# Attention on one core: probability sums moved behind the next group's value products, through a score-row bank and two sum buffers

## The reference

```python
x = x + xattn(layernorm(x), ctx, ctx)     # q (16,112,1024), k and v (16,375,256)
#   scores = q k^T / sqrt(32);  probs = softmax(scores);  out = (probs v) Wo
x = x + ffn(layernorm(x))                 # (silu(x w1^T) * (x w3^T)) w2^T
```

## Time and profile before

| | us |
|---|---|
| median of three executions (lowest, highest) | 2510.83 (2504.62, 2513.42) |
| span of the profiled execution, first to last instruction | 2511.5 |
| PE busy in that span | 2424.5 (97%) |
| DVE busy | 1727.6 (69%) |
| ACT busy | 979.1 (39%) |
| POOL busy | 576.1 (23%) |

### The profile page before, as it was taken

The page is one execution under the profiler, slowest core; times in us unless marked ns, Lnnn a source line. Parts: engine busy times, 40 slices in busy tenths (PEclk is TensorE's granted clock), DMA queues, the critical chain, the costliest instruction groups (busy, mean ns, idle before and its releaser), DMA issues.

```text
span 2511.5 us, 35414 instructions
## 1 busy us (share of the span) xinstructions
PE 2424.5 (97%) x12682; PEld 2069.3 (82%) x12682; DVE 1727.6 (69%) x2639; ACT 979.1 (39%) x1673; POOL 576.1 (23%) x305
## 2 busy tenths in 40 slices
PE   7998999999999699799999999999999989999999
PEld 7997878878876388699999988998899978888887
DVE  6425777777776446788888889898889874445442
ACT  3212445444454422444444445344443342323221
POOL 1000354454454400011111111332333320000000
PEclk9998999999998799899999999999999999999999
DMA  7534555455545345465655554666676687565652
GB/s 225 174 96 135 146 135 146 131 142 143 133 113 130 86 155 168 126 203 168 186 170 168 165 151 148 181 180 183 194 211 182 172 284 228 170 186 151 186 163 84
DMA packets 369146, 408.04 MB, mean 162 GB/s; under 512 B 125824, under 2 KB 324096, under 8 KB 359152
## 3 DMA queue, kind: packets, MB, share of 16 engines
q1 hardware_dynamic: 369008, 406.22, 56.7%
HBM read 252.99 MB, written 152.70 MB: 162 GB/s over the span
## 4 chain that ended last, share of the span: by engine, by line
PE 44%; DVE 9%; issue 3%; DMA 2%; ACT 0%; DVEq 0%; ACTq 0%
PE bank L84 15%; PE bank L85 15%; PE bank L86 15%; DVE g_WL L90 2%; DMA stash<-weight_scratch 2%; DVE g_su L1731 1%; DVE stash L1736 1%; DVE g_XL L90 1%; DVE stash L1228 1%; DVE stash L1226 1%; DVE xT L1723 1%; DVE stash L1225 1%; DVE stash L1249 0%; ACT g_XH L1659 0%; ACT g_WH L1198 0%
## 5 line engine op out<-in xcount | busy, mean ns | idle before, releaser
L84 PE MATMUL bank<-g_XH,g_WH 128*128 128x448 f32 (+1 forms) x2254 | 847.1, 376 | 30.2 <-DVE g_XL L90 15.9
L86 PE MATMUL bank<-g_XH,g_WL 128*128 128x448 f32 (+1 forms) x2254 | 845.0, 375 | 0.0
L85 PE MATMUL bank<-g_XL,g_WH 128*128 128x448 f32 (+1 forms) x2254 | 844.9, 375 | 0.0
L84 PEld LDWEIGHTS bank<-g_XH,g_WH 128*128 128x128 f32 x2254 | 424.5, 188 | 93.7 <-DVE g_WL L90 18.1
L86 PEld LDWEIGHTS bank<-g_XH,g_WL 128*128 128x128 f32 x2254 | 424.6, 188 | 55.3
L85 PEld LDWEIGHTS bank<-g_XL,g_WH 128*128 128x128 f32 x2254 | 424.7, 188 | 54.3
L90 DVE TENSOR_TENSOR g_WL<-stash,g_WH 128x512 fp32r<-128x512 f32 (+1 forms) x417 | 349.3, 841 | 75.8 <-ACT g_WH L1198 47.1
L1198 ACT ACTIVATE g_WH<-stash 128x512 fp32r<-128x512 f32 x392 | 241.7, 628 | 398.9 <-PE bank L86 245.1
L696 DVE TENSOR_REDUCE a_nm<-bank 112x1 f32<-112x375 f32 x512 | 264.9, 531 | 117.1 <-PE bank L831 113.8
L800 ACT ACTIVATE a_pr<-bank 125x448 f32<-125x448 f32 x384 | 204.0, 545 | 204.4 <-PE bank L907 150.8
L649 POOL TENSOR_TENSOR a_prsum<-a_pr 125x1792 f32<-125x1792 f32 x32 | 129.3, 4042 | 363.0 <-ACT a_pr L800 363.0
(11 more groups left out here) (132 smaller groups left out, 3617.8 us busy)
## 6 DMA issues: line engine op xcount, KB each, us to landing
stash<-in_L_ffn_w SPq DMA_DIRECT2D x168, 256.0 KB, 5.2
weight_scratch<-stash SPq DMA_DIRECT2D x28, 1024.0 KB, 7.6
stash<-weight_scratch SPq DMA_DIRECT2D x28, 1024.0 KB, 5.4
h_scratch<-g_Sh SPq DMA_DIRECT2D x112, 224.0 KB, 2.8
down_scratch<-xT SPq DMA_DIRECT2D x98, 256.0 KB, 3.0
stash<-in_ctx SPq DMA_DIRECT2D x48, 500.0 KB
stash<-h_scratch SPq DMA_DIRECT2D x25, 896.0 KB, 6.4
a_qst<-q_scratch SPq DMA_DIRECT2D x96, 224.0 KB, 4.7
```

The lines of the kernel that those rows point to most:

```text
L84: pe.matmul(acc, lh, rh, start=first, stop=False, skip_group_check=onto)
L85: pe.matmul(acc, lh, rl, start=False, stop=False, skip_group_check=onto)
L86: return pe.matmul(acc, ll, rh, start=False, stop=last, skip_group_check=onto)
```

## The change

- The sums of group 1 of the batch before are made in step 19, straight behind the value products of group 0; the sums of group 0 in step 31, straight behind those of group 1. On POOL's side `prsum` becomes two buffers, one per group, the second in a free part of `stash`.
- The sums go to `bank[1]`, one of the two score banks. Heads from 21 on swap banks, so that head 20 and head 31 sit in bank 0 when the sums are made. Heads 0 and 21 now wait for the head just before them, and heads 1 and 22 for `copy_sums`.
- ACT: `copy_sums` of group 0 goes to step 0 of the next turn, ahead of `copy_out` of group 1; that of group 1 to step 20, ahead of exponential 14 and `copy_out` of group 0.
- DVE inverts group 0's sums in steps 5, 8, 11, 14 of the next turn, group 1's in steps 22, 23, 25, 27.
- POOL scales group 0 of the batch before between the two adds of group 0, and group 1 behind them.
- SP: the store of group 0 goes behind the six loads of group 0's stacks (and so behind the `Wo` loads in turn 14), the store of group 1 behind the six loads of group 1's. The first load of the next stage waits for all sums, since its target overlaps the second `prsum`.

```diff
-                o_bank = l_bank = bank[6]
+                o_bank, l_bank = bank[6], bank[1]
-                SUMS = {2: (1, 1), 22: (0, 0)}
-                INV = {25: (0, 0), 27: (0, 1), 28: (0, 2), 31: (0, 3),
-                       5: (1, 0), 8: (1, 1), 11: (1, 2), 14: (1, 3)}
+                SUMS = {19: (1, 1), 31: (0, 0)}
+                HEAD_AFTER_SUMS = HEADS[19][-1] + 1
+                INV = {5: (0, 0), 8: (0, 1), 11: (0, 2), 14: (0, 3),
+                       22: (1, 0), 23: (1, 1), 25: (1, 2), 27: (1, 3)}
+                def head_bank(h):
+                    return s_bank[(h + (h >= HEAD_AFTER_SUMS)) % 2]
...
-                            if attn and not (isinstance(b, int) and b == 0):
-                                store(b - 1, 0)
                             if not isinstance(b, int) or -2 <= b < B - 4:
...
                                 load_stacks(i, par, b, 0)
                             if attn and not (isinstance(b, int) and b == 0):
-                                store(b - 1, 1)
+                                store(b - 1, 0)
                             if proj:
                                 load_stacks(i, par, b, 1)
+                            if attn and not (isinstance(b, int) and b == 0):
+                                store(b - 1, 1)
...
                         sp.wait_ge(pv_done, NC * NG * (B - 1))
+                        sp.wait_ge(sums_done, NG * B)
                         load_tile(sp, 0)
...
                                 add(b, 0, 0)
-                                if not (isinstance(b, int) and b == 0):
+                                if later:
+                                    scale(b - 1, 0)
+                                add(b, 0, 1)
+                                if later:
                                     scale(b - 1, 1)
-                                add(b, 0, 1)
                                 add(b, 1, 0)
                                 add(b, 1, 1)
-                                scale(b, 0)
...
-                                if attn and s == 1 and not (isinstance(b, int) and b == 0):
+                                if attn and s == 0 and not (isinstance(b, int) and b == 0):
+                                    copy_sums(b - 1, 0)
                                     copy_out(b - 1, 1)
-                                if attn and s - 1 in SUMS:
-                                    g, back = SUMS[s - 1]
-                                    if not (isinstance(b, int) and b < back):
-                                        copy_sums(b - back, g)
+                                if attn and s == 20 and not (isinstance(b, int) and b == 0):
+                                    copy_sums(b - 1, 1)
...
-                            pe.wait_ge(o_copied, NG * b + g + 1)
...
-                                                 prsum[:, r, :], start=True, stop=True)
+                                                 prsum[g][0:CK, r, :], start=True, stop=True)
...
-                                    wait(pe, max_done, NH * sb_ + h - 1)
+                                    wait(pe, max_done, NH * sb_ + h - (h not in (0, HEAD_AFTER_SUMS)))
+                                    if attn and h == 1:
+                                        wait(pe, l_copied, NG * b - 1)
+                                    if attn and h == HEAD_AFTER_SUMS + 1:
+                                        wait(pe, l_copied, NG * b)
...
                                     g = PV[s]
-                                    wait(pe, l_copied, NG * b + g)
+                                    wait(pe, o_copied, NG * b + g)
...
+                                    sg, back = SUMS[s]
+                                    if not (isinstance(b, int) and b < back):
+                                        if score:
+                                            pe.wait_ge(max_done, NH * sb_ + (20 if sg else NH - 1))
+                                        else:
+                                            pe.wait_ge(max_done, NH * (b + 1))
+                                        sums(b - back, sg)
```

More of the change, by code:

```diff
@@ L450, in attention @@
                 v = stash[0:CK, 8:10, 0:NC * KV].rearrange("p s (c n) -> p s c n", c=NC)
-                pr, prsum = sb("pr", [P, R, NC, J * SQ]), sb("prsum", [CK, R, J * SQ])
+                pr = sb("pr", [P, R, NC, J * SQ])
+                prsum = (sb("prsum", [CK, R, J * SQ]),
+                         stash[0:CK, 10:12, :].rearrange("p a n -> p (a n)")[:, 0:R * J * SQ]
+                         .rearrange("p (r n) -> p r n", r=R))
                 o, l = sb("o", [P, NG, J * SQ]), sb("l", [P, NG, J * SQ])
@@ L641, in add @@
                             n = NG * b + g
+                            acc = prsum[g][0:CK, :, :]
                             pool.wait_ge(exp_done, R * (NC * n + 2 + last))
@@ L644, in add @@
                                 pool.wait_ge(two_added, n + 1)
-                                pool.tensor_tensor(prsum[:], prsum[:], pr[0:CK, :, 2, :], ALU.add
+                                pool.tensor_tensor(acc, acc, pr[0:CK, :, 2, :], ALU.add
                                                    ).then_inc(all_added, 1)
                             else:
-                                wait(pool, sums_done, n)
-                                pool.tensor_tensor(prsum[:], pr[0:CK, :, 0, :], pr[0:CK, :, 1, :],
+                                wait(pool, sums_done, n - 1)
+                                if isinstance(b, int) and b == 0 and g == 1:
+                                    pool.wait_ge(w_lo, KT)
+                                pool.tensor_tensor(acc, pr[0:CK, :, 0, :], pr[0:CK, :, 1, :],
                                                    ALU.add).then_inc(two_added, 1)
@@ L661, in body @@
                             if attn:
+                                later = not (isinstance(b, int) and b == 0)
                                 add(b, 0, 0)
-                                if not (isinstance(b, int) and b == 0):
+                                if later:
+                                    scale(b - 1, 0)
+                                add(b, 0, 1)
+                                if later:
                                     scale(b - 1, 1)
-                                add(b, 0, 1)
                                 add(b, 1, 0)
                                 add(b, 1, 1)
-                                scale(b, 0)
                         each(pool, body)
+                        scale(B - 1, 0)
                         scale(B - 1, 1)
@@ L729, in body @@
                                                           ).then_inc(v_moved, 1)
[L730 to L735, removed]
+                                if attn and s in INV and not (isinstance(b, int) and b == 0):
+                                    invert(b - 1, *INV[s])
                         each(dve, body)
-                        for j in range(J):
-                            invert(B - 1, 1, j)
+                        for g in range(NG):
+                            for j in range(J):
+                                invert(B - 1, g, j)
                     @block.scalar
@@ L805, in _ @@
                         each(act, body)
+                        copy_sums(B - 1, 0)
                         copy_out(B - 1, 1)
@@ L910, in body @@
                                               ).then_inc(st_done, 1)
-                                if attn and s in SUMS:
-                                    g, back = SUMS[s]
-                                    if not (isinstance(b, int) and b < back):
-                                        sums(b - back, g)
                                 if attn and s in PV:
                                     g = PV[s]
-                                    wait(pe, l_copied, NG * b + g)
+                                    wait(pe, o_copied, NG * b + g)
                                     pe.wait_ge(v_moved, b + 1)
```

7 lines of the change are left out of this document (5 added, 2 removed).

## The result

The changed kernel takes **2588.32 us** (median of four runs, 2586.47 to 2593.84); the kernel before took 2510.97 us in four runs (2504.62 to 2513.42). The ratio is **1.0325, 95% interval 1.0307 to 1.0343**: slower by 77 us, 9 us less than forecast, inside the range. The profiled execution spans 2592.1 us, 80.6 more than before. The sum came out, but its terms did not: stall 1 was put too high and the clock far too low, and these errors cancelled in part.

A forecast was written before the change was run, and what follows sets the result against it. PE alone was taken to set the pace in attention's full turns. Terms 0 + 50 + 17 + 10 + 9 = 86 us, on the profiled 2511.5 us and less 0.7 for the median, gave 2597 us, range 2565 to 2640.

The forecast's parts named there:

- stall 1: Step 20, turns 1 to 12: group 0's `copy_out` waits for the late store, delaying head 26 by 4.2 us; 50 us.
- the clock: Turns 1 to 12: PE's idling brings half-clock stretches costing 1.7 us each; half of twelve, 10 us, bounds 0 and 40.
- stall 2: Step 0, turns 2 to 12: group 1's `copy_out` waits for its store, delaying head 6 by 1.5 us; 17 us.
- What the sums cost: Sums on PE, two per turn: 2.1 us falls to 1.64 behind the value products, gaining 0.46 us a turn.
- Heads 1 and 22: Heads waiting for `copy_sums`: head 1 loses 0.5 us, head 22 nothing, cancelling the sums' gain; 0 us a turn.
- POOL, DVE and the second buffer: Group 1's adds some 4 us later, covered by more than 5 us; attention's last load costs 0 to 1 us.
- the chain: Turn 8: store landing, `copy_out`, context copy, low part, maxima and inversion lead to head 26, 11.7 us behind the products' start.
- issued at 586.23: Turn 8: group 0's moved store, behind six loads, issues at 586.23 and lands 5.6 us later, at 591.8.
- The last turns: Turn 14: group 0's store behind the 32 `Wo` loads makes `copy_out` 9.3 us later; +9 us, bounds 0 and 12.
- only part of the halt reaches PE: Rival: PE feels ACT's halt through exponentials alone, 2 us in twelve turns, no clock loss; 2545 us, chance 0.22.
- Faster: Rival: group 0's store lands 2.4 us after issue, in time for step 20's `copy_out`; 2502 us, chance 0.07.
- No difference: Rival: PE slack absorbs the late copies, or waits removed at the end pay for half the stalls; 2511, chance 0.05.

The follow-up runs named there:

- x1: The changed kernel with group 0's store right behind the context load and POOL's scale of group 0 ahead of group 0's adds; 2542.8 us, ratio 1.0143.
- x3: The changed kernel with the edits of x1 and x2 together, so both stores early; 2524.67 us, ratio 1.0071.
- x5: The changed kernel with a second output buffer for group 0, by the batch's parity, all queue places kept; 2545.65 us, ratio 1.0154.
- x12: The changed kernel with x1's early store, a second output buffer for group 1, and group 1's inversions in steps 24, 25, 27, 28; 2502.71 us, ratio 0.9994.
- x13: x12 with head 1 of the next item moved behind step 1's projections; 2502.06 us, ratio 0.9982.
- x6: The kernel before with the context load issued ahead of group 0's store; 2503.05 us, ratio 0.9999.
- x2: The changed kernel with group 1's store ahead of the six loads of group 1's stacks; 2589.9 us, ratio 1.0331.
- x8: x3 with group 1's inversions in steps 24, 25, 27, 28 instead of 22, 23, 25, 27; 2532.8 us, ratio 1.0100.
- x10: x8 with both stores issued by POOL right behind its scaling; 2541.6 us, ratio 1.0139.

## Why the prediction was right, and where its terms were not

The total and its cause were right: 2597 forecast, 2588.32 measured, and experiments x1, x3, x5 and x12 show that the moved stores and what follows from them make nearly the whole loss, the rest being the inversions in steps 22 and 23. That the number came so close is in part luck: stall 1 was 17 us too high, the clock 22 us too low, stall 2 7 us too low. Against x12, which has the sums in the same place without the store waits and with the inversions spread, the twelve turns of the changed kernel split into idle time, 56.4 - 4.0 = 52.4 us, and the clock, 483.97 - 452.32 = 31.7 us. By the steps:

- **What the sums cost.** Forecast gain 0.46 us a turn, measured 5.1 / 12 = 0.42. Right. From the sums' start to the next head's they take 637.21 - 636.34 = 0.87 us.
- **Heads 1 and 22.** Forecast: head 1 loses 0.5 us and cancels that gain. Measured 3.2 / 12 = 0.27 in x12, and x13, which covers it, is 0.26 us a turn shorter. A wait on the weight load of up to 0.6 lies mostly beside the matmuls before it. With PE's other waits, which went from 2.0 to 0.8 us in the twelve turns, x12's turn is 0.26 us shorter than before, where 0 was forecast.
- **POOL, DVE and the second buffer.** At nothing, and nothing is seen. The prediction read the earlier trace rows as PE's own idle time, 30.2 us; PE's share was 11.6, the rest the weight loads'. It went to 3.6 us, and nothing came back for it at the end: turns 13, 14 and 15 (up to the next stage's first product) took 35.15, 31.74 and 43.6 us in x12, 110.5 together, and 110.8 in x13, against 35.47, 33.16 and 41.0 before, 109.6.
- **Stall 1: 4.2 us forecast, 2.75 measured** (head 26 at a mean of 10.31 us less 7.56), 33 us instead of 50. Every step of the chain holds: in turn 1 the store lands at 8.26 and head 26 starts at 11.74, where 8.2 and 11.7 were worked out. What failed is the step "issued at 586.23": it took the store's place from a turn in which the context load had delayed the key stores. In turns 2 to 12 the context load is issued earlier against them, the keys land in 3.1 us, and the store lands 6.4 to 7.0 us behind the value products. x6 shows this cause by itself in the kernel before, where the store in that place goes out 1.1 us earlier; x2 shows it the other way round.
- **Stall 2: 1.5 us forecast, 2.2 measured** (head 6 at a mean of 7.36 in turns 2 to 12, 5.16 in turn 1, where no store is due), 24 us instead of 17. The head's late place was nearly right (608.1 - 600.95 = 7.15); the unstalled place, 5.65, was not, in part since head 1's wait in it was 0.23 us too dear.
- **The clock: 10 us forecast, 31.7 measured**, inside its bounds of 0 to 40. A half-clock stretch costs the 1.7 us that rows 1 gave (x1), but there were 19 of 3.41 us in the twelve turns, not six: one to three in every turn. The step that failed is the count. Rows 1 held two examples, an idle stretch of nearly 4 us and one more than half busy, and waits such as the 1.35 and 0.73 us of turn 8 fall between them. Idle time alone does not give the count either: x1 with 36.1 us of it had five such stretches in the twelve turns, x5 with 35.6 one, x3 with 17.1 none. Only stall 1 was charged with a loss, and only half the time.
- **The last turns: 9 us forecast; turn 14 alone +10.0** (43.20 less 33.16), turns 0, 13 and 15 together -1.4: +8.6 for what lies outside turns 1 to 12.

From the first maxima transposes to the first product of the mixing stage attention takes 696.0 us against 606.4: +89.6, where the terms added up to 86. The whole is 80.6 us longer in the profiled executions. The stages behind attention, with the same code, took 10.6 us less from the first gate product on in this profile than in that of before (1459.2 against 1469.8); over the fourteen profiles this part varied from 1458.5 to 1469.8 us, so that difference is not the change's. The range, 2565 to 2640, was said to follow from the terms' bounds; these add up to 5 and 150 us, 2516 to 2661, so the narrower range was a judgment and not a sum.

Of the rivals, *only part of the halt reaches PE* falls: PE stands for DVE's maxima behind the low part, as argued against it, in 35 waits of up to 3.1 us. *Faster* falls with the landing times. *No difference* would need slack that PE does not have: x3, with 17 us of idle time, is already 0.7% slower.

## What to carry to other kernels

When a small store is moved in a DMA queue, ask for its landing, not its issue: behind a group of loads it lands after them, here even from a queue of its own, and the buffer it reads comes free only then. Put it where no transfer is under way, or give the buffer a twin; and look at what then stands behind the store, since a store that waits for its data delays each later issue (x8). Where one engine sets the pace, price short waits twice, once as waits and once as lost clock (here from nothing, in x3, to 31.7 us against 52.4 of waits), and compare with a version that has neither (x12): only there can the gain that a change was made for be read.

## What the runs showed of the hardware that was not expected

- A store issued on POOL's queue landed 0.5 us or more behind all loads that were already under way on SP's queue, 5.4 to 6.4 us after its issue (SP's own stores in that place: 5.2 to 6.1). In turns 2 to 12 of x10 its first packet moved 3.4 to 3.8 us after the issue, against 1.4 with nothing beside it.
- Two waits of 1.35 and 0.73 us in PE's work of turn 8 were followed by 3.42 us at 0.50, while a wait of 2.09 us in the same turn was followed by 3.58 us at 1.00. In x12 and x13, with 4.0 and 0.8 us of idle time in twelve turns, no stretch at 0.50 occurred in them.
- The context load of 3 x 500 KB is long: in turn 8 its packets ran until 14 us behind its issue (kernel before, x6 and changed kernel). Key stores issued 12 us behind it (kernel before) met its end, and the second landed 4.2 to 5.4 us after its own issue; some 14 us behind (x2 and x6), mostly 3.4 to 4.3; 14.6 us or more behind (the changed kernel, turns 2 to 11), 3.1. In x6 the store of `o` right behind the context load took 14 us to land. It is not the only thing that delays them: with group 0's store right ahead of them (x1, x12) the second took 5.1 to 5.5 us in turns 12 and 13, which have no context load; why stays open.
